# A two-layer graph attention and expert network on one core: a shorter inverse root in the layer norms, and the weighted sums of the second graph layer as whole-block products

## The reference

```python
def _layernorm(x, axis=-1, eps=1e-05):
    m = jnp.mean(x, axis=axis, keepdims=True)
    v = jnp.var(x, axis=axis, keepdims=True)
    return (x - m) / jnp.sqrt(v + eps)
...
x = x + _L0_gnn_ref(_layernorm(x), adj, W, a_src, a_dst)     # softmax over neighbours
x = x + _L0_ffn_ref(_layernorm(x), ...)                      # 2 of 8 experts, hidden 512
x = x + _L1_gnn_ref(_layernorm(x), adj, W, a)                # softmax over neighbours, then relu
x = x + _L1_ffn_ref(_layernorm(x), ...)                      # 2 of 8 experts, hidden 256
```

## Time and profile before

| what | value |
|---|---|
| median of 3 runs | 970.32 us |
| the profiled execution, its own time | 966.81 us |
| span of its trace | 965.0 us |
| DVE busy | 753.1 us (78%), 2881 instructions |
| PE busy | 662.5 us (69%) |
| POOL busy | 546.6 us (57%), 544 instructions |
| ACT busy | 479.1 us (50%) |
| scatters of the graph stages (line 448) | 256, 997 ns each |
| mean granted TensorE clock | 0.823 |

### The profile page before, as it was taken

The page is one execution under the profiler, slowest core; times in us unless marked ns, Lnnn a source line. Parts: engine busy times, 40 slices in busy tenths (PEclk is TensorE's granted clock), DMA queues, the critical chain, the costliest instruction groups (busy, mean ns, idle before and its releaser), DMA issues.

```text
span 965.0 us, 24021 instructions
## 1 busy us (share of the span) xinstructions
PE 662.5 (69%) x6281; PEld 552.2 (57%) x6282; DVE 753.1 (78%) x2881; ACT 479.1 (50%) x1065; POOL 546.6 (57%) x544
## 2 busy tenths in 40 slices
PE   3977677450999999998078878777208778778400
PEld 2755455350999999998066667666206656556300
DVE  6699999661899999998469989997517777787468
ACT  2466655410777777775146656664206555555200
POOL 0027777765376666767100666666664777777700
PEclk9998989755999999999568777777558998998755
DMA  8283333232233322326524544332333333333899
GB/s 223 81 198 105 104 103 109 75 113 59 67 94 86 86 82 85 87 78 173 142 59 134 140 131 140 89 89 68 93 92 93 99 102 100 97 101 98 224 237 285
DMA packets 168828, 111.51 MB, mean 116 GB/s; under 512 B 30306, under 2 KB 157737, under 8 KB 168776
## 3 DMA queue, kind: packets, MB, share of 16 engines
q1 hardware_dynamic: 151496, 77.04, 30.6%
q0 software_dynamic: 17280, 33.87, 10.6%
HBM read 60.32 MB, written 52.36 MB: 117 GB/s over the span
## 4 chain that ended last, share of the span: by engine, by line
PE 26%; issue 22%; POOL 21%; DVE 21%; DMA 5%; ACT 2%; SPq 1%; POOLq 1%; DVEq 0%; ACTq 0%
POOL row_buf L448 16%; PE bank L616 10%; PE bank L630 9%; POOL y_buf L456 5%; DVE xin L941 4%; DVE stat L886 3%; DVE x1w L993 2%; PE bank L602 2%; DMA y_buf<-g_y,g_dst 2%; PE bank L511 1%; DMA yin<-y_buf 1%; PE bank L528 1%; ACT xn L691 1%; DVE x1w L941 1%; PE bank L515 1%
## 5 line engine op out<-in xcount | busy, mean ns | idle before, releaser
L448 POOL DMA_INDIRECT row_buf<-pay,slot x256 | 255.2, 997 | 235.3 <-DVE slot L1062 155.8
L456 POOL DMA_INDIRECT y_buf<-g_y,g_dst x284 | 291.2, 1025 | 137.2 <-issue 89.9
L616 PE MATMUL bank<-g_xT,w 128*128 128x256 f16 x1278 | 171.4, 282 | 1.5 <-ACT g_xT L795 1.0
L795 ACT ACTIVATE g_xT<-bank 128x512 f16<-128x512 f16 x142 | 84.8, 597 | 170.0 <-PE bank L602 168.1
L616 PEld LDWEIGHTS bank<-g_xT,w 128*128 x1278 | 120.2, 101 | 21.0 <-issue 2.6
L602 PE MATMUL bank<-ident,g_in 128*128 128x128 f16 x568 | 58.3, 228 | 84.4 <-DMA g_in<-row_buf 71.7
L630 PE MATMUL bank<-w,g_h 128*128 x1260 | 86.3, 222 | 18.1 <-DVE g_y L1210 18.1
L802 ACT ACTIVATE xn<-bank,b_cols 128x256 f32<-128x256 f32 x216 | 86.7, 473 | 22.0 <-PE bank L616 15.5
L630 PEld LDWEIGHTS bank<-w,g_h 128*128 128x128 f16 x1260 | 77.8, 99 | 26.9 <-issue 24.7
L802 ACT ACTIVATE xt<-bank,b_cols 128x256 f32<-128x256 f32 x210 | 84.2, 474 | 16.1 <-PE bank L616 12.8
L602 PEld LDWEIGHTS bank<-ident,g_in 128*128 128x128 f16 x568 | 38.2, 102 | 92.4 <-issue 75.7
(11 more groups left out here) (184 smaller groups left out, 1363.0 us busy)
## 6 DMA issues: line engine op xcount, KB each, us to landing
g_in<-row_buf SPq DMA_DIRECT2D x142, 130.0 KB, 2.2
yin<-y_buf SPq DMA_DIRECT2D x24, 512.0 KB, 6.6
x_buf<-x1w SPq DMA_DIRECT2D x16, 520.0 KB, 4.5
xin<-x_buf SPq DMA_DIRECT2D x10, 520.0 KB, 5.6
y_buf<-g_y,g_dst POOLq DMA_INDIRECT x284
xin<-in_x_dram SPq DMA_DIRECT2D x8, 512.0 KB
adj_in<-in_adj_dram SPq DMA_DIRECT2D x16, 256.0 KB
row_buf<-pay,slot POOLq DMA_INDIRECT x256, 2.4
```

What stands on the lines that cost most here:

```text
L448: pool.indirect_dma_start(row_buf[L][:, :], bass.IndirectOffsetOnAxis(ap=slot[q][:, k, t:t + 1], axis=0), pay[q][:, t, :], None).then_inc( ...
L456: pool.indirect_dma_start(y_buf[L][:, :], bass.IndirectOffsetOnAxis(ap=g_dst[k][:, t:t + 1], axis=0), g_y[k][:, t, :], None, bounds_check= ...
L616: last = nc.tensor.matmul(dst, w[:, bass.ds(e * (2 * HID[L]) + (wp * HID[L] + c * P), P)], g_xT[q][:, xp, :], start=(m == 0), stop=(m == 2))
L795: nc.scalar.activation(g_xT[q][:, :, :], x_ps[q], ACT.Copy).then_inc(s.gT_sb, 1)
```

## The change

**The inverse root.** The variance term loses an instruction of its own (`mean`, line 893): the factor -0.5 moves into the last instruction. The constant EPS is added in the same instruction that forms the sum of squares where only one root is wanted; where two roots are wanted (st2 of layer 0) an instruction stays. The first guess is made by one multiplication of the bits by -0.5 and one addition, instead of a shift and a multiplication. The two refinement steps become a product of two quadratics of the same argument, which are evaluated side by side (`nt3`, `nt4`).

**The sums in layer 1.** `arrive` multiplies both expert results by their weights in one `tensor_tensor` of 2048 elements per partition (the weights broadcast over the features), and `take_in` adds the two products to x in two `tensor_tensor` of 1024 elements, with a wait ahead of each. `add_attention` multiplies `h_new` by `rinv` (broadcast) and adds x, in two instructions of 1024 elements with a wait between. In layer 0, where the attention result is in PSUM, it keeps its eight instructions. The last stage keeps `add_experts` as it was.

```diff
-DVE_SIGNALS = [98, 100]
+DVE_SIGNALS = [84, 88]
...
-                V.tensor_tensor(msum[:, :], stat[:, :, 1], stat[:, :, 4], ALU.add)
                 V.tensor_tensor(m2s[:, :], stat[:, :, 2], stat[:, :, 5], ALU.add)
                 ch.did(V.tensor_tensor(mdif[:, :], stat[:, :, 1], stat[:, :, 4], ALU.subtract))
+                V.tensor_tensor(msum[:, :], stat[:, :, 1], stat[:, :, 4], ALU.add)
                 pause()
-                V.tensor_scalar(mean[:, :], msum[:, :], -0.5, None, ALU.mult)
-                ch.did(V.tensor_tensor(mdif2[:, :], mdif[:, :], mdif[:, :], ALU.mult))
+                ch.did(V.scalar_tensor_tensor(mdif2[:, :], mdif[:, :], D / 4.0, mdif[:, :], ALU.mult, ALU.mult))
                 pause()
-                ch.did(V.scalar_tensor_tensor(m2s[:, :], mdif2[:, :], D / 4.0, m2s[:, :], ALU.mult, ALU.add))
+                if both is None:
+                    ch.did(V.scalar_tensor_tensor(ve[:, w], mdif2[:, :], EPS * D, m2s[:, :], ALU.add, ALU.add))
+                else:
+                    ch.did(V.tensor_tensor(m2s[:, :], mdif2[:, :], m2s[:, :], ALU.add))
+                    pause()
...
-                ch.did(V.tensor_scalar(half_bits[:, w], ve[:, w].bitcast(I32), 1, None, ALU.logical_shift_right))
+                ch.did(V.tensor_scalar(nt1[:, w].bitcast(I32), ve[:, w].bitcast(I32), -0.5, RT_BITS, ALU.mult, ALU.add))
                 pause()
-                ch.did(V.tensor_scalar(nt1[:, w].bitcast(I32), half_bits[:, w], -1.0, float(0x5f3759df), ALU.mult, ALU.add))
-                pause()
-
                 ch.did(V.tensor_tensor(nt2[:, w], nt1[:, w], nt1[:, w], ALU.mult))
                 pause()
                 ch.did(V.tensor_tensor(nt2[:, w], nt2[:, w], ve[:, w], ALU.mult))
                 pause()
-                ch.did(V.scalar_tensor_tensor(nt3[:, w], nt2[:, w], -10.0 / 3.0, nt2[:, w], ALU.add, ALU.mult))
+                V.scalar_tensor_tensor(nt3[:, w], nt2[:, w], RT_B[0], nt2[:, w], ALU.add, ALU.mult)
+                ch.did(V.scalar_tensor_tensor(nt4[:, w], nt2[:, w], RT_A[0], nt2[:, w], ALU.add, ALU.mult))
                 pause()
-                ch.did(V.scalar_tensor_tensor(nt1[:, w], nt3[:, w], 5.0, nt1[:, w], ALU.add, ALU.mult))
-                pause()
-
-                ch.did(V.tensor_tensor(nt2[:, w], nt1[:, w], nt1[:, w], ALU.mult))
-                pause()
-                ch.did(V.scalar_tensor_tensor(nt2[:, w], nt2[:, w], -0.5 * 0.375 ** 3 * D ** 0.5, ve[:, w], ALU.mult, ALU.mult))
+                ch.did(V.scalar_tensor_tensor(nt3[:, w], nt3[:, w], RT_B[1], nt1[:, w], ALU.add, ALU.mult))
                 pause()
                 root = rstd if both is None else both
-                ch.did(V.scalar_tensor_tensor(root[:, w], nt2[:, w], 1.5 * 0.375 * D ** 0.5, nt1[:, w], ALU.add, ALU.mult))
+                ch.did(V.scalar_tensor_tensor(root[:, w], nt4[:, w], RT_A[1], nt3[:, w], ALU.add, ALU.mult))
...
-                return V.tensor_tensor(nmr[:, :], mean[:, :], rstd[:, 0:TILES], ALU.mult)
+                return V.scalar_tensor_tensor(nmr[:, :], msum[:, :], -0.5, rstd[:, 0:TILES], ALU.mult, ALU.mult)
...
@@ arrive
-                    add_experts(xin[q], [yin[q][:, k, :, :] for k in range(TOP)], (0,))
+                    weights = xin[q][:, :, 0:TOP].rearrange("p t k -> p k t").unsqueeze(3).to_broadcast([P, TOP, TILES, D])
+                    ch.did(V.tensor_tensor(yin[q][:, :, :, :], yin[q][:, :, :, :], weights, ALU.mult))
@@ take_in
-                    ch.wait()
-                    ch.did(add_experts(xin[q], [yin[q][:, k, :, :] for k in range(TOP)], (1,)))
+                    for k in range(TOP):
+                        ch.wait()
+                        ch.did(V.tensor_tensor(xin[q][:, :, X_AT:X_END], xin[q][:, :, X_AT:X_END], yin[q][:, k, :, :], ALU.add))
                     ch.wait()
@@ add_attention, layer 1
+                    ch.did(V.tensor_tensor(h_new[:, :, :], h_new[:, :, :],
+                                           rinv[:, :].unsqueeze(2).to_broadcast([P, TILES, D]), ALU.mult))
+                    ch.wait()
+                    last = V.tensor_tensor(x1w[q][:, :, X_AT:X_END], h_new[:, :, :], xin[q][:, :, X_AT:X_END], ALU.add)
```

More of the change, by code:

```diff
@@ L46 @@
 BIG = 3.0e38
+RT_BITS = 1598872064.0
+RT_A, RT_B = (-5.454677581787109, 8.706277847290039), (-1.1617217063903809, 2.8224129676818848)
 IDLE_EXP, IDLE_ATT = [10, 0], [7, 8]
@@ L166, in gnn_moe_kernel @@
         stat = sb("stat", [P, TILES, 6])
-        msum, mdif, m2s, mdif2, mean = (sb(n, [P, TILES]) for n in ("msum", "mdif", "m2s", "mdif2", "mean"))
-        ve, nt1, nt2, nt3 = (sb(n, [P, 2 * TILES]) for n in ("ve", "nt1", "nt2", "nt3"))
-        half_bits = sb("half_bits", [P, 2 * TILES], I32)
+        msum, mdif, m2s, mdif2 = (sb(n, [P, TILES]) for n in ("msum", "mdif", "m2s", "mdif2"))
+        ve, nt1, nt2, nt3, nt4 = (sb(n, [P, 2 * TILES]) for n in ("ve", "nt1", "nt2", "nt3", "nt4"))
         rstd1, nmr1 = sb("rstd1", [P, TILES]), sb("nmr1", [P, TILES])
@@ L888, in statistics @@
                 pause()
[L889 removed]
                 V.tensor_tensor(m2s[:, :], stat[:, :, 2], stat[:, :, 5], ALU.add)
                 ch.did(V.tensor_tensor(mdif[:, :], stat[:, :, 1], stat[:, :, 4], ALU.subtract))
+                V.tensor_tensor(msum[:, :], stat[:, :, 1], stat[:, :, 4], ALU.add)
                 pause()
[L893 to L894 removed]
+                ch.did(V.scalar_tensor_tensor(mdif2[:, :], mdif[:, :], D / 4.0, mdif[:, :], ALU.mult, ALU.mult))
                 pause()
[L896 to L907 removed]
+                if both is None:
[3 more added lines that the diff above has]
+                    pause()
+                    w = slice(0, 2 * TILES)
+                    V.tensor_scalar(ve[:, 0:TILES], m2s[:, :], EPS * D, None, ALU.add)
+                    ch.did(V.tensor_scalar(ve[:, TILES:], m2s[:, :], 1.0 + EPS, EPS * EPS * D, ALU.mult, ALU.add))
+                pause()
+                ch.did(V.tensor_scalar(nt1[:, w].bitcast(I32), ve[:, w].bitcast(I32), -0.5, RT_BITS, ALU.mult, ALU.add))
                 pause()
@@ L935, in finish_steps, with add_experts @@
                     ch.wait()
-            def add_experts(src, y, part=range(TOP)):
-                for k in part:
+            def add_experts(src, y):
+                for k in range(TOP):
                     for t in range(TILES):
@@ L944, in add_experts @@
                         ch.did(last)
-                        if len(part) == 2:
-                            ch.wait()
+                        ch.wait()
                 return last
@@ L990, in add_attention @@
                 dve.wait_ge(s.rinv_ready, n + 1)
-                for t in range(TILES):
-                    att = att_tile[L][t][:, 0:width] if L == 0 else h_new[:, t, :]
-                    last = V.scalar_tensor_tensor(x1w[q][:, t, X_AT:X_AT + width], att, rinv[:, t:t + 1],
-                                                  xin[q][:, t, X_AT:X_AT + width], ALU.mult, ALU.add)
+                if L == 0:
+                    for t in range(TILES):
+                        last = V.scalar_tensor_tensor(x1w[q][:, t, X_AT:X_AT + width], att_tile[L][t][:, 0:width], rinv[:, t:t + 1],
+                                                      xin[q][:, t, X_AT:X_AT + width], ALU.mult, ALU.add)
+                else:
+                    ch.did(V.tensor_tensor(h_new[:, :, :], h_new[:, :, :],
+                                           rinv[:, :].unsqueeze(2).to_broadcast([P, TILES, D]), ALU.mult))
+                    ch.wait()
+                    last = V.tensor_tensor(x1w[q][:, :, X_AT:X_END], h_new[:, :, :], xin[q][:, :, X_AT:X_END], ALU.add)
                 last.then_inc(s.x_done, 1)
```

6 lines of the change are left out of this document (removed).

## The result

The changed kernel takes 964.34 us (median of 4 runs, 963.83 to 964.75) against 970.5 us (median of 4, 967.79 to 972.44) for the kernel before on the same chip: a ratio of 0.9937, interval 0.9916 to 0.9958. It is faster by 0.6%. The forecast was 963.1 us, in a range of 958 to 968.5.

A forecast was written before the change was run, and what follows sets the result against it. POOL was taken to bound layer 0 after its first slots, DVE layer 1. Layer 0's -1.2 us and layer 1's -6.05 us gave -7.25: from 970.32 to 963.1 us, range 958 to 968.5.

The forecast's parts named there:

- Which engine sets the pace: Graph stages: POOL's scatters in layer 0 after its first slots; DVE in layer 1, busy 22.72 of 23.97 us per block.
- The sums, +0.64 us per block: Layer 1's whole-block sums cost DVE 0.64 us per block; bounds -1.1 (whole durations count) and +3.8 (broadcast halves the rate).
- rivals 3 and 4: Layer 1's sums: whole durations count, 955 us, 4%; or products with a broadcast operand run at half rate, 985.5 us, 4%.
- The root, -0.88 and -0.45 us: Layer 1's shorter root saves DVE 0.88 us per block in st2 and 0.45 us in st1, beside `route`.
- The jump, -2.4 us: Layer 1's DVE loop, 240 rows instead of 298: the gap where it jumps back goes, saving 2.4 us; bounds 0 and 2.4.
- Rival 1: Layer 1's loop jump: the gap stays, or another like it comes elsewhere; gain only 4.85 us, 965.5 us; 17%.
- x in time: `arrive` in layer 1: x lands about 4.3 us after `x_done`, `arrive` would start at 4.9, leaving 0.6 us of room.
- Rival 2: Layer 1: x lands 5.8 us after `x_done`, so st2's saving is waited away in six blocks; 968.3 us; 9%.
- Layer 1 together: Layer 1's first block, five more blocks, jump and last steps: -6.05 us at POOL's block 6, then nothing added or lost.
- Layer 0, -1.2 us, "POOL carries it to the end of the stage": Layer 0: shorter roots ahead of the first slots save 1.2 us, between 0.9 and 1.5, kept to the stage's end.
- Rival 5: A loss as large as the gain from something unseen, such as a lower granted clock in PE's layer 1 part; 968; 6%.
- POOL's wait of 2.9 us: Layer 1: POOL's waits at block starts would be about 2.9 us, where block 1 had 3.57 us.

The follow-up runs named there:

- e2: Kernel before with only the new whole-block sums of layer 1, old root in both layers: 972.19 us, ratio 1.0016 to the kernel before.
- e1: Kernel before with only the shorter root in both layers, old sums in layer 1: 958.94 us, ratio 0.9872 to the kernel before.
- e3: Changed kernel with 30 semaphore increments behind the product in both steps of layer 1's loop, 300 rows: 967.38 us, ratio 0.9955 to the kernel before.
- e5: e1 with ten instead of seven idle TensorE products behind layer 0's attention: 955.70 us, ratio 0.9856 to the kernel before.

## Why the prediction was right, point by point

- **Which engine sets the pace.** Right in layer 1. In layer 0 "whatever DVE saves there after the first slots is worth nothing" has a counterpart that was missed: in the kernel before, the slots of blocks 1 to 6 were ready only 1.6 to 4.5 us before POOL could use them, and what delays them by more costs at once.
- **The sums, +0.64 us per block.** Measured +0.68 from the rows and about +0.6 from e2. The bounds of -1.1 and +3.8 are both excluded, and with them rivals 3 and 4. The rule of the Trainium skill, "VectorE: DVE Perf Modes", section "The DRAIN you can't avoid", that the next instruction waits until the pipe is empty would have made the sums a gain. The same section adds that a next instruction that is not held starts earlier, which the prediction left out. The trace agrees with that addition: the eight rows of 0.35 us start every 0.275 us.
- **The root, -0.88 and -0.45 us.** Measured -0.86 and -0.43, and -1.25 for the block in e1. Alone, in the first block of layer 1, the chain runs from 478.81 (`m2s`) to 480.78 (`nmr`), 1.97 us; forecast 1.99.
- **The block, 23.3 us.** Measured 23.3.
- **The jump, -2.4 us.** Right, and e3 brings the gap back with 60 more rows, where the prediction had only two loops to go by. Rival 1 is out for this kernel; its case that the place of the code and not its length decides is not excluded.
- **x in time.** Right: DVE's only wait for x in layer 1 is 0.4 us, for block 2, where the prediction has x late too. Rival 2 is out. Its 4.3 us from `x_done` to the landing are not what its rows give, 629.9 - 626.1 = 3.8 us, so there was more room than it said. Where the prediction had 1.35 us to spare for `h_new`, blocks 1 to 6 have 0.46 to 1.44 now.
- **Layer 1 together.** Forecast: -6.05 us up to block 6's scatters, about -0.5 of it in the first block. Measured: -0.74 ahead of the first scatter and -5.50 from there to block 6's, -6.24 together.
- **Layer 0, -1.2 us, "POOL carries it to the end of the stage".** This step failed. The first scatter did come 1.53 us earlier, but the stage ended 0.58 us later, 2.1 us lost on the way. The two new waits cost 4.2 us beyond the usual 0.30 between two scatters, and a stop ahead of the last block, which the trace puts down to no engine, 0.6 more (3.00 us instead of 2.42; the prediction's "from scatter to scatter until the stage ends" passed over it). Against that the 128 scatters were 2.6 us shorter in sum (984 ns on average instead of 1004). Rival 5 named a lower granted clock as a possible loss, but put it in layer 1 and at 6%; it came in layer 0. In e5, where POOL waits for no slots but its first, the gain is carried: first scatter 1.3 us earlier than before, the last one's end 1.9.
- **POOL's wait of 2.9 us.** Wrong: 0.99 us. The waits were reckoned with scatters as long as before, and they became longer. It changed no total.

In sum the graph stages gained 5.8 us in the traces where 7.25 were forecast, and the medians differ by 6.2. That these two agree proves little: the whole spans of the two traces differ by only 2.8 us, and which of the two the 3.4 us between traces and medians belong to is not known. The forecast of the total is 1.2 us off although one of its terms had the wrong sign, since that term was small.
